# Exchanged rotary halves of the latent queries: from a matrix product to four SBUF transfers of a sine product

## The reference, cut to what matters

```
q_c    = q @ W_dq                         # 96 latents for each token
q_rope = (q_c @ W_qr)                     # 16 heads of 64
def _rope(x, L):                          # x1, x2: first and second 32 of the 64
    return concatenate([x1*cos - x2*sin, x1*sin + x2*cos])
scores = (q_nope . k_nope + rope(q_rope) . rope(k_rope)) * scale
```

## Time and profile before

| | us |
|---|---|
| time, median of 3 runs | 699.65 (698.43 to 701.21) |
| the profiled execution's own time | 701.32 |
| its span, first to last instruction | 699.3 |
| PE busy | 655.2 (94%) |
| DVE busy | 478.2 (68%) |
| ACT busy | 352.4 (50%) |
| POOL busy | 355.7 (51%) |

### The profile page before, as it was taken

How to read it: one execution, slowest core, us unless ns; L and a number is a source line. 1 busy time by engine, 2 the same in 40 slices (tenths; PEclk the granted TensorE clock), 3 DMA queues, 4 the chain that set the end, 5 groups by cost and what they waited for, 6 DMA issues and landing times.

```text
span 699.3 us, 12881 instructions
## 1 busy us (share of the span) xinstructions
PE 655.2 (94%) x4654; PEld 517.1 (74%) x4654; DVE 478.2 (68%) x1103; ACT 352.4 (50%) x813; POOL 355.7 (51%) x481
## 2 busy tenths in 40 slices
PE   8989989889998888889999999999999999999995
PEld 6856668858676645567788888887579888888884
DVE  5579868493174899998866856775365655566656
ACT  4655536150544746346887877776352222222224
POOL 5326416671101887545786756766434444444431
PEclk9999999999999999899999999999999999999999
DMA  8000007001003000000000100000102111111001
GB/s 284 2 2 3 1 2 300 1 1 50 0 1 86 1 16 0 2 1 1 1 1 2 69 1 2 1 2 1 68 24 68 38 53 46 46 46 46 0 1 61
DMA packets 10352, 23.32 MB, mean 33 GB/s; under 512 B 2033, under 2 KB 5074, under 8 KB 9906
## 3 DMA queue, kind: packets, MB, share of 16 engines
q1 hardware_dynamic: 10002, 22.24, 9.4%
q10 hardware_dynamic: 288, 0.26, 0.1%
HBM read 21.45 MB, written 1.05 MB: 32 GB/s over the span
## 4 chain that ended last, share of the span: by engine, by line
PE 72%; DVE 19%; ACT 4%; issue 2%; POOL 1%; DMA 1%; POOLq 0%; SPq 0%; DVEq 0%; ACTq 0%
PE psum L463 43%; DVE A L1555 6%; PE psum L1126 4%; PE psum L1137 4%; PE psum L524 4%; DVE A_rounded L1480 2%; PE psum L577 2%; PE psum L946 2%; PE psum L619 1%; DVE A L1404 1%; DVE stats L1277 1%; DVE x_tok L1274 1%; PE psum L788 1%; PE psum L583 1%; PE psum L593 1%
## 5 line engine op out<-in xcount | busy, mean ns | idle before, releaser
L463 PE MATMUL psum<-parts 128*128 128x256 f32 (+2 forms) x1472 | 253.7, 327 | 3.1 <-DVE C L1591 1.1
L463 PEld LDWEIGHTS psum<-parts 128*128 128x128 f32 (+1 forms) x1472 | 219.9, 190 | 32.3 <-issue 4.0
L2213 POOL TENSOR_SCALAR probs<-probs,row_rec 128x256 f32<-128x256 f32 x128 | 69.9, 558 | 47.6 <-DVE row_rec L1348 44.6
L2126 ACT ACTIVATE A<-psum 128x512 f32<-128x512 f32 x44 | 26.3, 598 | 115.6 <-PE psum L463 115.5
L1798 ACT ACTIVATE probs<-probs,neg_max 128x256 f32<-128x256 f32 x128 | 63.7, 500 | 32.9 <-DVE neg_max L1339 32.9
L1674 DVE TENSOR_TENSOR A<-A,psum 128x512 f32<-128x512 f32 x44 | 30.1, 687 | 70.6 <-ACT A L2126 58.4
L1555 DVE TENSOR_TENSOR_SCAN A<-decay,psum 128x256 f32<-128x256 f32 x128 | 75.4, 662 | 4.3 <-PE psum L946 4.3
L1339 DVE CUSTOM_DVE_ANT_0 probs<-psum,ctxT 128x256 f32<-128x256 f32 x128 | 48.9, 419 | 38.9 <-PE psum L463 36.8
L463 PE MATMUL psum<-parts,A_rounded 128*128 128x256 f32 x404 | 65.3, 288 | 3.5 <-DVE A_rounded L1480 3.5
L463 PEld LDWEIGHTS psum<-parts,A_rounded 128*128 128x128 f32 x404 | 56.3, 196 | 4.9 <-DVE A_rounded L1480 2.8
L1712 DVE TENSOR_TENSOR parts<-A,parts 128x512 fp32r<-128x512 f32 x44 | 48.9, 1111 | 0.1
(11 more groups left out here) (270 smaller groups left out, 1283.2 us busy)
## 6 DMA issues: line engine op xcount, KB each, us to landing
A<-in_experts SPq DMA_DIRECT2D x12, 384.0 KB, 3.1
C<-in_experts SPq DMA_DIRECT2D x10, 384.0 KB, 3.0
A<-in_w_o SPq DMA_DIRECT2D x1, 2048.0 KB, 12.8
x_tok<-in_x_tok SPq DMA_DIRECT2D x1, 1024.0 KB, 7.2
ctxT<-in_ctxT SPq DMA_DIRECT2D x1, 1024.0 KB, 10.9
A<-in_w_uqT SPq DMA_DIRECT2D x1, 768.0 KB, 6.8
out<-x_tok SPq DMA_DIRECT2D x6, 128.0 KB, 1.8
xT<-in_xT SPq DMA_DIRECT2D x2, 256.0 KB, 3.8
```

The costliest lines, as they stand in the source:

```text
L463: ins = mm(o, left[l], right[r], start=first and n == 0, stop=last and n == 2, skip_group_check=True)
L2213: last = pool.tensor_scalar(pr, pr, row_rec[:, u % RING[n], j:j + 1], 1.0, ALU.mult, ALU.mult)
```

## The change

A constant `PLAIN` = 5 is added. For pairs n < 5 nothing is changed but the order of the two multiplications. For pairs n of 5 and more (27 pairs) PE makes no exchanged rows. DVE multiplies the raw rows with the sine table into a new buffer `sine_part` and raises `q_sine`, then with the cosine table. SP waits for `q_sine`, and for the transfers of the pair before, and issues four transfers from SBUF to SBUF of 32 partitions by 256 floats (32 KB) each, which put the halves of the sine product in exchanged places of `ropes`; each raises `q_swap` by 16. POOL waits for all four and subtracts in place of adding, since the table's sign belongs to the other half now.

The schedule moves with it: queries of pair n are made at u = max(n, 2n - 6) in place of 2n - 4 (4, 5, 6, 8, 10, ... in place of 4, 6, 8, 10, ...), and POOL's `add_pair` at one unit later than that for n of 5 and more, u = 2n - 5 from n = 7 on. The exchanged weights are loaded and split for 5 heads' pairs in place of 8, in two POOL steps in place of three. The loads of the first three expert chunks come on SP behind pair 20's transfers. Some semaphores are put together, with counts to match (`qk` and `v`, `m_g` and `m_u`, `warm` and `const_p`).

```diff
-        QUERIES_AT = {2 * (n - FIRST) + 4: n for n in range(FIRST, B * NPAIR)}
+        QUERIES_AT = {max(n, 2 * n - 6): n for n in range(FIRST, B * NPAIR)}
+        ADDED_AT = {u + (n >= PLAIN): n for u, n in QUERIES_AT.items()}
+        QUARTERS = ((0, 32), (32, 0), (64, 96), (96, 64))
+        RAW_BEHIND = 20
...
+            def swap_halves(n):
+
+                sp.wait_ge(sem("q_sine"), n - PLAIN + 1)
+                if n > PLAIN:
+                    sp.wait_ge(sem("q_swap"), 64 * (n - PLAIN))
+                for to, at in QUARTERS:
+                    sp.dma_start(ropes[to:to + 32, n % 2, S:2 * S], sine_part[at:at + 32, n % 2, :]
+                                 ).then_inc(sem("q_swap"), 16)
...
+            for n in range(PLAIN, B * NPAIR):
+                swap_halves(n)
+                if n == RAW_BEHIND:
+                    sp.wait_ge(sem("fin"), 4 * NT + 1)
+                    for c in range(RAW - 1):
+                        load_expert(c)
+            sp.wait_ge(sem("a4_av"), B * NPAIR)
...
-                product3(rope[:, 0:S], left(wqr_raw_parts), rhs, True, True)
-                product3(rope[:, S:2 * S], left(wqr_swp_parts), rhs, True, True).then_inc(sem("q_rope"), 1)
+                last = product3(rope[:, 0:S], left(wqr_raw_parts), rhs, True, True)
+                if n < PLAIN:
+                    last = product3(rope[:, S:2 * S], left(wqr_swp_parts), rhs, True, True)
+                last.then_inc(sem("q_rope"), 1)
...
-                tt(ropes[:, n % 2, 0:S], rope[:, 0:S], tab_qc, ALU.mult)
-                tt(ropes[:, n % 2, S:2 * S], rope[:, S:2 * S], tab_qs, ALU.mult).then_inc(sem("q_mul"), 1)
+                if n < PLAIN:
+                    tt(ropes[:, n % 2, S:2 * S], rope[:, S:2 * S], tab_qs, ALU.mult)
+                else:
+                    tt(sine_part[:, n % 2, :], rope[:, 0:S], tab_qs, ALU.mult).then_inc(sem("q_sine"), 1)
+                tt(ropes[:, n % 2, 0:S], rope[:, 0:S], tab_qc, ALU.mult).then_inc(sem("q_mul"), 1)
...
                 pool.wait_ge(sem("q_mul"), n + 1)
+                if n >= PLAIN:
+                    pool.wait_ge(sem("q_swap"), 64 * (n - PLAIN + 1))
+                signed = ALU.add if n < PLAIN else ALU.subtract
...
-                if u in QUERIES_AT:
-                    if u:
-                        pool.wait_ge(sem("a4_norm"), u)
-                    add_pair(QUERIES_AT[u])
+                if u in ADDED_AT:
+                    pool.wait_ge(sem("a4_norm"), u)
+                    add_pair(ADDED_AT[u])
```

More of the change, by code:

```diff
@@ L75, in build @@
         A_rounded = sb("A_rounded", [P, 16384], f32r)
+        with nc.sbuf_tensor("parts_plain", [P, 10752], f32) as parts_plain:
+            pass
         parts = sb("parts", [P, 10752], f32r)
@@ L209, in build @@
         wqr_raw = view(C, 3584, [QC, NPAIR, P])
-        wqr_swp = view(C, 4608, [QC, NPAIR, P])
+        wqr_swp = view(C, 4608, [QC, PLAIN, P])
         w_dq = view(C, 5632, [P, DC, QC])
@@ L218, in build @@
         wqr_raw_parts = view(parts, 0, [QC, 2, NPAIR, P])
-        wqr_swp_parts = view(parts, 2048, [QC, 2, NPAIR, P])
+        wqr_swp_parts = view(parts, 2048, [QC, 2, PLAIN, P])
+        sine_part = view(parts_plain, 3328, [P, 2, S])
         qk_parts = view(parts, 4096, [QC, 2, NPAIR, P])
@@ L442, in _, with load_expert @@
             load("tab_qs", tab_qs)
[L443 to L446, removed]
+            def swap_halves(n):
[5 more added lines that the diff above has]
+                                 ).then_inc(sem("q_swap"), 16)
+            def load_expert(c):
+                sp.dma_start(raw[c % RAW], d["experts"][c]).then_inc(sem(f"ld_raw{c % RAW}"), 16)
+            for n in range(PLAIN, B * NPAIR):
[5 more added lines that the diff above has]
+            sp.wait_ge(sem("a4_av"), B * NPAIR)
+            for c in range(RAW - 1, FCH):
                 if c >= RAW:
                     sp.wait_ge(sem("m_wd"), c - RAW + 1)
-                sp.dma_start(raw[c % RAW], d["experts"][c]).then_inc(sem(f"ld_raw{c % RAW}"), 16)
+                load_expert(c)
             for i in range(NT - 2):
@@ L560, in heads_of_tile @@
                                     [wqk_parts[:, r, dc, :] for r in range(2)], dc == 0, dc == DC - 1)
-                last.then_inc(sem("qk"), 1)
+                last.then_inc(sem("qkv"), 1)
                 if i == 0:
@@ L568, in heads_of_tile @@
                                     [wv_parts[:, r, dc, :] for r in range(2)], dc == 0, dc == DC - 1)
-                last.then_inc(sem("v"), 1)
+                last.then_inc(sem("qkv"), 1)
             def row_scores(o, qt):
@@ L649, in _ @@
                     loaded(pe, "ident")
-                    pe.wait_ge(sem("const_p"), 1)
+                    pe.wait_ge(sem("const_p"), 2)
                 if i >= 2:
@@ L813, in mixing @@
                 if k < 2:
-                    pe.wait_ge(sem("const_p"), 4)
+                    pe.wait_ge(sem("const_p"), 5)
                     pe.wait_ge(sem("f_alTs"), k + 1)
@@ L1033, in _ @@
                     if n == 5:
-                        pe.wait_ge(sem("const_p"), 3)
+                        pe.wait_ge(sem("const_p"), 4)
                     state_sums(n // 4 - 1)
@@ L1168, in product_to @@
                                     [x_parts[:, r, dc, hh] for r in range(2)], dc == 0, dc == DC - 1)
-                last.then_inc(sem(("m_g", "m_u")[w]), 1)
+                last.then_inc(sem("m_gu"), 1)
             def gate_up(place):
@@ L1360, in rotate @@
             def rotate(i):
-                dve.wait_ge(sem("qk"), i + 1)
+                dve.wait_ge(sem("qkv"), 2 * i + 1)
                 if i >= 2:
@@ L1670, in product_of_tile @@
                 dve.wait_ge(sem("m_silu"), place + 1)
-                dve.wait_ge(sem("m_u"), place + 1)
+                dve.wait_ge(sem("m_gu"), 2 * place + 2)
                 if k >= AHEAD:
@@ L1822, in _ @@
                 if i == 0:
-                    act.wait_ge(sem("const_p"), 1)
-                act.wait_ge(sem("v"), i + 1)
+                    act.wait_ge(sem("const_p"), 2)
+                act.wait_ge(sem("qkv"), 2 * i + 2)
                 af(v_sum[:, i, :, 0:HD0], bank[2 + i % 2][:, 0:D].rearrange("p (h w) -> p h w", w=HD0), ACT.Copy
@@ L2121, in silu @@
             def silu(place):
-                act.wait_ge(sem("m_g"), place + 1)
+                act.wait_ge(sem("m_gu"), 2 * place + 1)
                 if place >= 2:
@@ L2347, in _ @@
                         last.then_inc(sem("q_split"), 1)
[L2348 to L2351, removed]
+                if n == 25:
+                    link(pool.tensor_copy(wqr_swp_parts[:, 0], wqr_swp))
+                if n == 26:
+                    pool.tensor_tensor(wqr_swp_parts[:, 1], wqr_swp, wqr_swp_parts[:, 0].bitcast(f32),
+                                       ALU.subtract).then_inc(sem("q_split"), 1)
                 if n == 24:
@@ L2384, in split_weights @@
                 if c >= 2:
-                    pool.wait_ge(sem("m_u"), 3 if c == 2 else 2 * c - 2)
+                    pool.wait_ge(sem("m_gu"), 6 if c == 2 else 4 * c - 4)
                 link(pool.tensor_copy(gu_parts[:, c % 2, 0, :], w[:, 0:GU]))
```

16 lines of the change are left out of this document (8 added, 8 removed).

## The result

| us | before | after |
|---|---|---|
| median of the runs (lowest to highest) | 699.84 (698.43 to 701.21), 4 runs | 693.00 (692.59 to 693.44), 4 runs |
| the profiled execution's own time | 701.32 | 692.59 |
| its span | 699.3 | 690.8 |
| PE busy | 655.2 | 645.5 |

The ratio is 0.9899, with an interval from 0.9871 to 0.9927: faster by 1.0%, 6.8 us. The forecast was 690.4, 2.6 us lower. A second set of runs of the changed kernel on another chip gave 692.31 (6 runs) beside 700.48 (17 runs), 8.2 us, ratio 0.9891 [0.9867, 0.9914].

What follows compares the result with a forecast made beforehand. PE was taken to bound the attention, its chain holding PE alone. Removed matmuls -9.63 us and the start +0.4 gave -9.2, so 699.65 became 690.4 us; range 688.3 to 696.5.

Steps and rivals of the forecast that it cites:

- the forecast proper: Whole kernel: 690.4 us, with 688.3 to 692.5 covering scan-stage gain and spread of the runs; given 71%.
- Rival 1: Attention's start and short stretches: DVE or ACT take over, costing 1.5 and 1.8 us, 693.3 us in all; 14%.
- Rival 2: Attention's swap: four transfers land one behind the other, 7.6 us, stretching short pairs of units; 695.7 us; 7%.
- the prediction's own signs: Attention: POOL's DMA wait at most 1 us a pair; PE's queries waiting over 1.5 us, 325 to 340, means wrong.
- The price of a matmul: Attention queries on PE: 0.119 us a matmul, three fewer for each of 27 pairs, 9.63 us gained.
- The start of the attention: Units up to 8: one pair more in work while DVE and ACT are full; 0.4 us lost, bounds 0 to 1.5.
- The transfers: Attention's sine swap: last landing 3.5 us after the sine product (L), hidden; cost 0, bounds 0 to 2 us.
- The margin: Attention: PE feels transfers from L = 5.8 us, ACT from 4.9; SP's own wait never late at L = 3.5.
- Rival 3: Attention: the swap becomes the loop's clock, pair length (L + 2.6) / 2, 5.7 us; slower, 706.2 us; 4%.
- POOL's single split of the exchanged weights: Scan stage: POOL's splitting shrinks to 5/8, by some 1.3 us; counted 0, bounds 0 to 1.3 us gained.
- The three expert loads: SP's queue: moved behind pair 20, they cost 0, or once a microsecond within POOL's margin.
- The median: Whole kernel: median of the runs taken 1.67 us below the profiled execution, so 692.1 profiled becomes 690.4 us.

Runs made afterwards that it cites:

- the change from pair 8: The changed kernel, but pairs 4 to 7 keep their old units and matmuls, exchanged weights split for eight pairs in three steps: 691.28 us, ratio 0.9869.
- schedule alone: The kernel before with only the new units for queries and additions, all matmuls kept, no transfers: 701.02 us, ratio 1.0011.
- A second bank: The changed kernel with pair 5's latents in PSUM bank 4 in place of bank 5, PE's waits adjusted: 691.77 us, ratio 0.9869.
- six transfers: The changed kernel with two more 16 KB transfers ahead of each pair's four, into a place nobody reads: 700.92 us, ratio 1.0008.

## Why the prediction was right, and where it was not

**The sum as a whole.** The measured 693.00 lies above the 692.5 with which the forecast proper ended, and in the part of the range that was left to rivals 1 and 2. Rival 1 said 693.3, but only its half at the start came true, so its nearness is luck. Two of the prediction's own signs came out against it: POOL waits 1.3 us a pair for the DMA, up to 2.4, where 1 was the most, and PE's queries wait 1.8 us for ACT between 325 and 340 us, where more than 1.5 was to mean wrong. ACT's split of a pair (L2114, L2085 before) waited once, 1.1 us.

**The price of a matmul: right.** 0.119 us from the chain, not 0.283 from the group: 9.35 us less behind unit 11 where 9.26 was due, 1.98 to 1.62 us in an even unit, and 8.63 for 8.57 in the change from pair 8.

**The start of the attention: right place, mis-sized term.** I took 0.4 us with bounds 0 to 1.5; the runs show 2.0 (schedule alone) and 2.2 to 2.3 (the change). With 2.3 the forecast would have been 692.3, against 693.0 and 692.3. I had named both banks, and had asked whether DVE and ACT are full. The narrower thing decided most of it: ACT does its work of a unit in a written order, exponentials first and the latents' copy behind them, so a single bank is not free before late. In the changed kernel the copies of pairs 4 and 5 end 3.1 and 3.3 us behind the start of these pairs' matmuls, while a unit is about 2.5 us long. With pairs in every second unit PE has a unit in between; with pairs 4, 5 and 6 in units 4, 5 and 6 it has none. PE's rows and ACT's row that ends each wait, in the changed kernel:

```profile
327.14 0.98 PE L487 MATMUL psum<-parts 96*128 96x256 f32 x6 [0.64 <-ACT A L2043]
330.45 0.97 PE L487 MATMUL psum<-parts 96*128 96x256 f32 x6 [1.18 <-ACT A L2043]
```

```profile
325.84 0.49 ACT L1827 ACTIVATE probs<-probs,neg_max 128x256 f32<-128x256 f32 x1
326.33 0.36 ACT L2042 ACTIVATE A<-psum 64x256 f32<-64x256 f32 x1
326.70 0.38 ACT L2043 ACTIVATE A<-psum 64x256 f32<-64x256 f32 x1
...
329.12 0.62 ACT L2114 ACTIVATE A_rounded<-A 128x512 fp32r<-128x512 f32 x1
329.64 0.37 ACT L2042 ACTIVATE A<-psum 64x256 f32<-64x256 f32 x1
330.02 0.38 ACT L2043 ACTIVATE A<-psum 64x256 f32<-64x256 f32 x1
```

In the second, exponentials and the splitting of a pair (0.62 us) stand ahead of the copy. The two waits are 1.8 of the 2.3 us. A second bank took them away and brought 1.2 us, since 0.7 us of other waits came in their place. So the one bank was the first of two things there. That DVE and ACT are close to full is the other is argued from these waits and not tried, and about 0.5 us of the loss stands in no wait of PE's.

**The transfers: right that they are hidden, and near in size.** L was put at 3.5 us, 1.3 for four issues and 2.2 to land. Pair 17's neighbours around 390 us, in the timeline (the sine product, then POOL's addition):

```profile
388.61 0.41 DVE L1619 TENSOR_TENSOR parts_plain<-psum,ctxT 128x256 f32<-128x256 f32 x1
392.97 0.86 POOL L2346 TENSOR_TENSOR A<-C 64x256 f32<-64x256 f32 x1 [1.63 <-DMA C<-parts_plain]
```

L is 392.97 - 389.02 = 3.95 us, to the start of POOL's addition. An issue takes 0.59 us where the loads' 0.33 to 0.43 were taken, and from an issue's start to its landing pass 1.8 us (median of 108) where the tables' 2.2 was taken. Three issues at 0.63 us from start to start and one landing are 3.7 us; the rest is hand-over:

```profile
C<-parts_plain SPq DMA_DIRECT2D x108, 32.0 KB, 1.8
```

Rival 2 falls with that: four in line at 1.8 us would be 7.2. The rule of the Trainium skill's page "DMA: Bandwidth & Descriptors", section "Rules for kernel authors", that two transfers to disjoint partition halves serialize and that one should not bother, does not hold here for the time to the last landing of these four 32 KB transfers, each of 32 partitions: they overlap but for their issues. No run here shows whether it holds for large ones.

**The margin: wrong.** The step said that PE first feels the transfers at L = 5.8 us, ACT at 4.9, and that SP's own wait is never late. The last is so only for four transfers. SP waits for a batch's landing before it issues the next, so its queue is a loop of its own, and at six transfers that loop (5.0 us and more) passes the short pairs. Then L is no longer issues and one landing, for SP comes to a pair's transfers late. For the pair whose sine ended at 386.27, SP issued at 387.36 and POOL added at 392.55: L was 6.3 us, and 7.1 for the pair before, where the experiment had put 5.1. Both are over the step's 5.8, so the runs do not refute its thresholds; what failed is SP's wait, which it put at nothing from L = 3.5 us alone. Six transfers cost 8.6 us beside the changed kernel on the same chip (700.92 - 692.31). Rival 3 had the right kind of mechanism, the swap as clock of the loop, but the wrong formula: (L + 2.6) / 2 with POOL's work in it, in place of the issues and one landing.

**Nothing else moved.** DVE 478.2 us before and after. POOL's single split of the exchanged weights is one piece of 1.55 us (288.98) in place of two of 1.26, behind a copy of 0.71 in place of 1.03; no gain of it reached the end, and no loss can be told. The three expert loads behind pair 20 hold nobody up: PE is full through 340 to 460 us. Rival 1 gets a part, at the start; its short stretches of 4.23 us show no wait of PE.

**The median: partly luck.** The 1.67 us from the profiled execution to the median stay unexplained. One dip of the granted clock costs the profile of before 1.5 us against that of after (13.28 for 11.80 us; the clock was 0.50 of full speed, the level of 1.2 GHz, from 127 to 129 us, and 1.00 after). But the profile of the kernel with the second bank has the dip as well and is the quickest of its five runs, 690.17 with a median of 691.77. For the changed kernel's profiled execution the prediction had 692.1, and 692.59 was measured. That is nearer than the terms were: the start cost 1.9 us more than taken, and the missing dip gave 1.5 back.

## What to carry to other kernels

Price a removed matmul by two otherwise equal units in the chain, and then ask of every unit whose order changes which single buffer it shares with its new neighbour and where in the other engine's written order that buffer is emptied. A queue that waits for its own landings before the next batch is a loop with a period of its own, issues plus one landing; hold it against the shortest stretch between two batches, not the mean one. Where a schedule has to be pulled forward to cover a new latency, try to begin after the crowded units: here the three pairs left as they were cost 1.1 us and the crowding 2.3.

## What the runs showed of the hardware

- An issue of a 32 KB transfer from SBUF to SBUF on SP takes 0.59 us, and 1.8 us pass from its start to its landing (medians of 108); the issues are in line, the landings overlap. The transfers of 16 KB took as long, 0.59 and 1.8 us (medians of 54, the kernel with six).
- PE was idle for 2.40 to 2.42 us ahead of the same 96 matmuls in all twelve profiles. In seven the granted clock then dropped and they took 13.1 to 13.3 us (before: 0.61 from 126 to 129 us, between full speed and the level of 1.2 GHz); in five they took 11.8 (after: 1.00). The two profiles of the changed kernel differ in this, 11.80 and 13.09 us. So a difference of 1 us between two spans is first to be looked for there.
